# Two-block gated cross-attention network: another order of the engines' work in the fused last stage, and other PSUM banks for two transposes

## The reference, cut to what matters

```python
# attention: 16 heads of 64, scores over the 64 rows of the same sequence's context
fq, fk, fv = q @ w_q, k @ w_k, v @ w_v            # q is layernorm(x); k, v are the context
ps = softmax(fq fk^T / 8 + mask)
x = x + tanh(g) * ((ps fv) @ out_w.T + out_b)
# feed-forward
xq = round(x_n * scale) / scale                   # scale = 127 / max|x_n| of the row, x_n = layernorm(x)
h  = silu(depthwise_conv3(xq @ w1q.T))            # along the 64 rows; 512 hidden features
x  = x + tanh(g) * (quantised(h) @ w2q.T)         # h is rounded by its own row's step
```

## Time and profile before

| | before |
|---|---|
| three executions, us | 1636.68, 1643.49, 1648.65 |
| profiled execution, us | 1640.07 |
| span of it, us | 1637.7 |
| PE busy, share of the span | 92% |
| DVE busy | 72% |
| ACT busy | 61% |
| POOL busy | 42% |
| the fused stage | from about 752 us to the end |

### The profile page before, as it was taken

One profiled execution on the slowest core, in us unless ns is written; L12 is line 12 of the kernel. 1 busy time (PEld: TensorE's weight loads), 2 busy tenths in 40 slices (PEclk: granted clock), 3 DMA queues, 4 the chain that ended last, 5 costly groups with the idle time before them and its releaser, 6 DMA issues.

```text
span 1637.7 us, 51409 instructions
## 1 busy us (share of the span) xinstructions
PE 1505.6 (92%) x20222; PEld 1246.3 (76%) x20222; DVE 1174.8 (72%) x3120; ACT 995.8 (61%) x2018; POOL 692.5 (42%) x611
## 2 busy tenths in 40 slices
PE   5999999999839999997899999999999999999988
PEld 2777777777729999986677777777787878888864
DVE  5788878876544222234587989889898899888875
ACT  3787777766214444443456566766666667767756
POOL 2234667575441111144565454444444444333320
PEclk9899999987559999998999999999999999999999
DMA  9999950000038888861000000000000000000000
GB/s 299 393 387 386 382 196 24 24 31 21 27 113 257 263 267 262 255 196 39 26 23 18 18 17 22 24 22 22 23 23 22 22 22 22 12 16 12 14 9 23
DMA packets 97661, 173.36 MB, mean 106 GB/s; under 512 B 12320, under 2 KB 44960, under 8 KB 97168
## 3 DMA queue, kind: packets, MB, share of 16 engines
q1 hardware_dynamic: 84816, 144.05, 26.3%
q0 software_dynamic: 11600, 25.65, 4.6%
q10 hardware_dynamic: 1008, 0.40, 0.1%
HBM read 79.41 MB, written 90.64 MB: 104 GB/s over the span
## 4 chain that ended last, share of the span: by engine, by line
PE 39%; DVE 8%; issue 4%; ACT 1%; POOL 1%; another core or an unknown queue 0%; DVEq 0%; ACTq 0%
PE L1psY L1283 6%; PE L1psY L1290 6%; PE L1psM L1332 5%; PE L1psY L1275 5%; PE L1psT L1324 4%; PE L1psS L1301 4%; PE L1psT L1310 2%; DVE L1sc L1708 1%; PE L1psF L1380 1%; PE L1psF L1361 1%; PE L1psF L1398 1%; DVE L1den L1719 1%; DVE L1am L1770 1%; PE L1psM L1390 1%; DVE x L1600 1%
## 5 line engine op out<-in xcount | busy, mean ns | idle before, releaser
L1851 POOL TENSOR_TENSOR L1sc<-L1sc,L1top 128x1024 f32<-128x1024 f32 x64 | 121.8, 1904 | 240.8 <-DVE L1top L1715 240.8
L1463 ACT ACTIVATE L1KT<-L1psY 128x512 f32<-128x512 f32 x128 | 78.0, 609 | 226.7 <-PE L1psY L1275 216.9
L1004 ACT ACTIVATE GhT<-GpsH,Gwx 128x256 f32<-128x256 f32 (+1 forms) x312 | 117.9, 445 | 149.9 <-PE GpsH L972 143.6
L855 POOL TENSOR_TENSOR L0sc<-L0sc,L0top 128x1024 f32<-128x1024 f32 x64 | 121.6, 1900 | 178.6 <-DVE L0top L564 177.7
L1856 POOL TENSOR_TENSOR L1sc<-L1sc,L1rden 128x1024 f32<-128x1024 f32 x64 | 121.8, 1904 | 177.0 <-DVE L1rden L1724 177.0
L1283 PE MATMUL L1psY<-L1xnT,L1WQ 128*128 128x128 f32 x1024 | 142.8, 283 | 1.0 <-ACT L1xnT L1458 1.0
L1021 DVE TENSOR_TENSOR yg<-GpsY,Gwx 128x256 f32<-128x256 f32 (+1 forms) x78 | 30.3, 389 | 158.0 <-PE GpsY L980 84.9
L861 POOL DMA_INDIRECT rows_in<-L0xr,slot x128 | 124.5, 972 | 45.3 <-issue 31.8
L1275 PE MATMUL L1psY<-cx,L1WK 128*128 128x128 f32 x1024 | 138.4, 279 | 2.6 <-DVE L1identh L1791 2.5
L980 PE MATMUL GpsY<-Gwx,GhT 128*128 128x128 f32 x1080 | 133.1, 275 | 0.0
L980 PEld LDWEIGHTS GpsY<-Gwx,GhT 128*128 128x128 f32 x1080 | 130.9, 192 | 2.7
(11 more groups left out here) (326 smaller groups left out, 3732.4 us busy)
## 6 DMA issues: line engine op xcount, KB each, us to landing
Gwx<-in_experts SPq DMA_DIRECT2D x78, 579.0 KB, 4.3
rows_in<-L0zero SPq DMA_DIRECT2D x1, 33792.0 KB, 92.7
rows_out<-L0zero SPq DMA_DIRECT2D x1, 33792.0 KB
Gxg<-rows_in SPq DMA_DIRECT2D x57, 128.0 KB, 3.8
rows_out<-yg POOLq DMA_DIRECT2D x57, 128.0 KB
cx<-in_ctxT SPq DMA_DIRECT2D x64, 64.0 KB
out<-X SPq DMA_DIRECT2D x64, 64.0 KB, 1.7
L0ctxT<-in_ctxT SPq DMA_DIRECT2D x1, 2560.0 KB, 18.6
```

The costliest lines, as they stand in the source:

```text
L855: nc.gpsimd.tensor_tensor(sc[:, t % 4, :, :], sc[:, t % 4, :, :], top[:, t % 2, :].unsqueeze(2).broadcast_to([P, H, S]), ALU.subtract).the ...
L1004: nc.scalar.activation(hT[:, u, m, 0:blocks(t) * P], psH[:, u, m, 0:blocks(t) * P], ACT.Gelu, bias=wx[:, w, ob1 + m:ob1 + m + 1]).then_inc ...
L1851: nc.gpsimd.tensor_tensor(sc[:, t % SR, :, :], sc[:, t % SR, :, :], broad(top[:, t % 2, :]), ALU.subtract).then_inc(s["shifted"], 1)
```

## The change

Nothing is computed differently. In the fused stage five things change.

- ScalarE: `exps` moves ahead of both `take_probs`, which now stand together behind it. `centre` goes behind the first `take_q`, and `tanh` ahead of the second `take_o`.
- VectorE: `add_x`, `largest` and `scales` open the next round instead of closing this one (the neighbours stay the same, as the rows below show). `residual` goes behind `add_bias` instead of ahead of it, `scale` ahead of `layernorm`, and `layernorm` behind `sums` and `invert`. The last three portions of small steps stand behind `twice_silu`.
- GpSimd: `fetch` stands behind `normalise` in every round. Before, this was so only in rounds 0 to 5.
- TensorE: `turn_xq` and `turn_steps` of the 14 groups in integers write into the two banks of the scores (`psS`) instead of `psM` and `psF`, and stand behind `project_out`. They wait for `add_bias` of the round, and the next `scores` waits for ScalarE's copies of both.
- TensorE: `project_out` waits for the halves of its input one by one.

```diff
             if stage == "xq":
-                return ("M", psM[:, 2:4, :]) if t // G4 < INT_GROUPS else ("F", psF[:, :])
+                return ("S", flat(psS[:, 0, :, :])) if t // G4 < INT_GROUPS else ("F", psF[:, :])
+            if stage == "steps":
+                return "S", flat(psS[:, 1, :, :])
...
             def scores(t):
                 pe.wait_ge(s["q_ready"], 2 * t + 2)
                 wait(pe, s["scores_out"], t)
+                g = min((t + LX - FX - 1) // G4 + 1, INT_GROUPS)
+                wait(pe, s["xqT_ready"], g)
+                wait(pe, s["steps_ready"], g)
...
             def project_out(t):
-                pe.wait_ge(s["OT_ready"], 2 * t + 2)
                 take_bank("M", s["x_new"], t + 1)
                 for i in range(HP):
+                    if i % 4 == 0:
+                        pe.wait_ge(s["OT_ready"], 2 * t + i // 4 + 1)
...
             def turn_xq(g):
...
-                take_bank(name, s["xqT_ready"], g + 1)
                 if g < INT_GROUPS:
+                    pe.wait_ge(s["scores_out"], min(G4 * g + FX - LX + 1, NT))
                     ps = halves(ps, BF16)
+                else:
+                    take_bank(name, s["xqT_ready"], g + 1)
...
# TensorE's loop
-                if k >= FX and (k - FX) % G4 == 0 and k - FX < NT:
+                if k >= FX and (k - FX) % G4 == 0 and INT_GROUPS <= (k - FX) // G4 < NG:
                     turn_xq((k - FX) // G4)
-                if k >= FX and (k - FX) % G4 == 0 and (k - FX) // G4 < INT_GROUPS:
-                    turn_steps((k - FX) // G4)
                 if tt is not None:
                     project_out(tt)
+                if k >= FX and (k - FX) % G4 == 0 and (k - FX) // G4 < INT_GROUPS:
+                    turn_xq((k - FX) // G4)
+                    turn_steps((k - FX) // G4)
...
# ScalarE's loop
-                if tt is not None:
-                    take_probs(tt, 0)
                 if tile(k - 1, FT) is not None:
                     rounding(tile(k - 1, FT))
                 if tx is not None:
                     take_xnT(tx)
+                if tv is not None:
+                    exps(tv)
                 if tt is not None:
+                    take_probs(tt, 0)
                     take_probs(tt, 1)
                 if tx is not None:
                     take_k(tx, 1)
-                if tv is not None:
-                    exps(tv)
...
# GpSimd's loop
-                if k >= 6:
-                    for t in fetches.get(k, []):
-                        fetch(t)
                 if tv is not None:
                     normalise(tv)
-                if k < 6:
-                    for t in fetches.get(k, []):
-                        fetch(t)
+                for t in fetches.get(k, []):
+                    fetch(t)
```

More of the change, by code:

```diff
@@ L1349, in turn_steps @@
                 pe.wait_ge(s["xq_ready"], g + 1)
-                take_bank("F", s["steps_ready"], g + 1)
+                ps = bank("steps", G4 * g)[1]
                 for i in range(G4):
                     t = G4 * g + i
-                    last = nc.tensor.transpose(psF[:, i * P:(i + 1) * P], inv[:, t:t + 1].broadcast_to([P, P]), ident[:])
+                    last = nc.tensor.transpose(ps[:, i * P:(i + 1) * P], inv[:, t:t + 1].broadcast_to([P, P]), ident[:])
                 last.then_inc(s["steps_ps"], 1)
@@ L1502, in take_steps @@
                 wait(act, s["h_scaled"], FM * (g - 1))
-                nc.scalar.activation(step[:, g % 2, :], psF[:, :], ACT.Copy).then_inc(s["steps_ready"], 1)
+                nc.scalar.activation(step[:, g % 2, :], bank("steps", G4 * g)[1], ACT.Copy).then_inc(s["steps_ready"], 1)
             def centre(n):
@@ L1552, in _ @@
                     take_k(tx, 1)
-                if tv is not None:
-                    exps(tv)
+                if tx is not None:
+                    take_q(tx, 0)
                 if n is not None:
                     centre(n)
-                if tx is not None:
-                    take_q(tx, 0)
                 if tt is not None:
@@ L1562, in _ @@
                     take_q(tx, 1)
+                if n2 is not None:
+                    tanh(n2)
                 if tt is not None:
                     take_o(tt, 1)
-                if n2 is not None:
-                    tanh(n2)
                 if tb is not None:
@@ L1794, in _ @@
                 n, n2, th, tb = tile(k, FH), tile(k, FH + 1), tile(k, FT), tile(k, FB)
+                if tile(k - 1, LT) is not None:
+                    add_x(tile(k - 1, LT))
+                if tile(k - 1, FT) is not None:
+                    largest(tile(k - 1, FT))
+                    scales(tile(k - 1, FT))
                 if to is not None:
@@ L1799, in _ @@
                 small(k, 0)
+                if n is not None:
+                    scale(n)
+                small(k, 1)
+                if tv is not None:
+                    sums(tv)
+                    invert(tv)
                 if tile(k, LN) is not None:
@@ L1802, in _ @@
                 if n is not None:
-                    scale(n)
-                small(k, 1)
-                small(k, 2)
-                if tv is not None:
-                    sums(tv)
-                    invert(tv)
-                if n is not None:
                     conv_left(n)
                     conv_right(n)
-                small(k, 3)
                 if n2 is not None:
                     twice_silu(n2)
+                small(k, 2)
+                small(k, 3)
                 small(k, 4)
+                if tx is not None:
+                    add_bias(tx)
                 if tb is not None:
@@ L1818, in _ @@
                 if tx is not None:
-                    add_bias(tx)
                     tops(tx)
-                if tt is not None:
-                    add_x(tt)
-                if th is not None:
-                    largest(th)
-                    scales(th)
+            add_x(NT - 1)
+            largest(tile(LAST - 1, FT))
+            scales(tile(LAST - 1, FT))
             LAST_NORM = {50: range(11, 18), 51: range(18, 23), 52: range(23, FFN_OPS)}
```

## The result

| | before | changed |
|---|---|---|
| median (lowest to highest) | 1641.5 us (1636.7 to 1648.7), 4 runs | 1693.4 us (1686.9 to 1701.3), 4 runs |
| span of the profiled execution | 1637.7 | 1688.4 |
| ratio | | 1.031 (1.027 to 1.035) |

The account below looks back on a forecast made before the run. TensorE bounds the kernel, 12.07 us a tile plus waits. Middle: -23.1 - 7.2 + 11.6 + 37.4 = +18.7; nine tiles before +7.1, 14 behind +2.2: +28 on 1640.07, predicted 1667 us, range 1620 to 1690 (own range 1655 to 1685).

Parts of the forecast that it names:

- The step that failed: Fused stage, tiles 0 to 5: given no term in the sum, so predicted difference 0.
- The tail: Fused stage, tile 63 to the end: given no term in the sum, so predicted difference 0.
- Gathers on the scores: Middle tiles: both gathers now hit the scores, 1.1 us each in 34 tiles, +37.4 us (30 to 79).
- Gathers away from `values`: Middle tiles: gathers issued behind `normalise` no longer interrupt `values`, 0.89 us off 26 tiles, -23.1 us.
- `exps` ahead of the copies: ScalarE: copies of the probabilities end later, `values` starts at 4.53 instead of 4.19; 34 tiles at 0.34, +11.6 us.
- Banks for integers and steps: Middle's eight turning rounds: the steps' wait for `residual` goes, 1.6 us becomes 0.7 each, -7.2 us.
- the shorter way to the maxima: VectorE, `residual` behind `add_bias`: maxima end about 2.75 us after the scores instead of 3.19.
- Rival 3: VectorE's `twice_silu` delays the gathers 0.7 us, hitting scores for 1.8 us instead of 1.1: +30, 1697 us; 5%.
- the rule: Skill's shared-port rule: gathers beside `twice_silu` would come later and longer; left out of the sum as not borne out.
- Rivals 1, 2 and 4: Scores not hurt, 1624 us, 22%; price about half a microsecond, 1641 us, 17%; gathers and ScalarE's order free, 1604 us, 4%.
- rival 4: Fused stage: neither the gathers nor ScalarE's order cost anything, `exps` having unseen slack; 1604 us; 4%.

## Why the prediction was right in direction and wrong in size

With the two kernels on both kinds of chip the difference splits into what small matmuls lose to gathers (hurt chip less spared chip) and the rest (changed less before, spared chip). These are single profiles of different chips; the second changed profile on a hurt chip repeats the first one within 0.6 us a stretch.

| us | tiles 0 to 5 | 6 to 14 | 15 to 48 | 49 to 62 | 63 to the end |
|---|---|---|---|---|---|
| before, spared chip | 70.6 | 104.4 | 433.8 | 175.1 | 79.2 |
| changed, spared chip | 73.6 | 110.1 | 437.2 | 177.2 | 81.2 |
| the rest | +3.0 | +5.7 | +3.4 | +2.1 | +2.0 |
| gathers, before | 7.2 | 6.2 | 12.3 | -0.8 | -2.5 |
| gathers, changed | 19.9 | 8.9 | 30.9 | 0.0 | -0.6 |

The last two columns have few gathers or none; their differences show how far two chips or profiles differ anyway.

**The step that failed** is the one that isn't in the sum: the prediction starts its parts at tile 6 and takes the first six tiles as unchanged, without a reason. They cost +15.7 us, over two thirds of what the forecast (28) fell short of the measured 50.7. GpSimd gathers four times a round there. The place of these gathers in its own order is the same in both kernels; it is the other engines' new order that brings them forward, from 10.2 us or more of the tile to 7.7 to 8.1 in tiles 3 and 4, so that they lie on the scores from their start. Scores of 3.5 to 4.7 us stand in three of the six tiles, where the earlier trace rows show the one such case before (the stage's first tile has 6.4 us before and 6.5 now). The waits were accompanied by the granted clock's falls, 34 us at the lower level instead of 10. Of the 15.7, 12.7 are gathers and the clock with them: on the spared chip the changed kernel's mean granted clock is 0.95 in these tiles, on the two hurt ones 0.82 and 0.85. On one hurt chip the same kernel takes 92.9 us there with gathers and 69.9 with plain DMAs at their place. Which engine's order brings them forward was not separated on a hurt chip. The miss of 22.7 us is these 15.7, the tail's 4.0, also not in the sum, and 5.2 in the parts that were in it, less 2.2 us by which the part ahead of the stage was shorter. (The sum itself gives 1640.07 + 28.0 = 1668 us; the prediction has 1667.)

The tail, too, stood at nothing. In the round that drains the pipeline `values` waits for the late copy, and behind that idle time the clock is at its lower level for 3.4 us, and again later for 6.8 (`values` takes 1.99 us at it instead of 1.16):

```profile
1624.76 1.99 PE L1329 MATMUL L1psT<-L1PT,L1V 64*64 64x64 f32 x64 [1.67 <-ACT L1PT L1493]
```

**Gathers on the scores**: predicted for every tile, 1.1 us each. Right: they hit in every one of tiles 15 to 48. The price is about 1.0, 1.1, 1.8 (or 1.4) and 0.9 (or 0.7) in the four kinds of round, 1.13 on average, 38.5 us in all. The plain tile is 13.5 us with gathers and 12.46 without, as forecast (13.5 and 12.4). GpSimd's pair runs from 7.7 to 10.0 us in a plain tile (8.2 to 10.4 in the forecast). The largest price is in the round in which it ends 1.1 us later (11.14).

**Gathers away from `values`**: predicted -23.1, a loss counted by adding the gaps of 26 tiles. The measurement is -12.3: on the spared chip, with every `values` whole, the kernel before still needs 433.8 us. Its four kinds of round are 12.06, 12.07, 12.6 or 13.2, and 14.05 to 14.3 us there; without the gap in `values` the third kind is no shorter (12.91 us on average, 12.95 on the hurt chip) and the fourth gains 0.5 of the 0.9 (14.13, 14.62), so something else ends those tiles, and the gap had lain in that wait. The same is seen on the scores: the gaps add up to 38.5 us, close to the forecast's 37.4, but the difference between the chips is 30.9. The two errors were +10.8 and -6.5 us; that the middle came out at +22.0 against +18.7 owes something to their cancelling.

**`exps` ahead of the copies**: predicted 0.34 a tile, measured 0.40 (`values` at 4.59, not 4.19), TensorE's largest named wait in the middle (19.2 us of idle time at 34 places). ScalarE's whole new order, alone on a spared chip, costs 13.4 us there, predicted 11.6.

**Banks for integers and steps**: predicted -7.2 in the middle. The turning tile gains 0.45 of the 0.9 and on a hurt chip gives most of it back to `values` one tile later. VectorE's order was given no price of its own beyond the shorter way to the maxima; the whole of it, alone, costs 7.8 us in the middle and 6.4 in tiles 49 to 62. In the changed kernel the three together are +3.4, about the +4.4 that the prediction had for them, and far less than the 21.2 us that the two orders cost one by one: each is cheaper beside the other.

**Rival 3, gathers held back by `twice_silu`.** The forecast called it not borne out by the trace. It exists, at a smaller price; that the measured 1693 us lies near this rival's 1697 is a coincidence. GpSimd's gathers and VectorE's `twice_silu` in the changed kernel, first GpSimd, then VectorE:

```profile
1150.04 1.26 POOL L1878 DMA_INDIRECT yr<-rows_out,slot  x1
...
1205.03 1.32 POOL L1878 DMA_INDIRECT yr<-rows_out,slot  x1
```

```profile
1149.44 1.00 DVE L1773 SCALAR_TENSOR_TENSOR L1hs<-L1hs,L1hc 128x512 f32<-128x512 f32 x1
...
1204.80 0.69 DVE L1773 SCALAR_TENSOR_TENSOR L1hs<-L1hs,L1hc 128x512 f32<-128x512 f32 x1 [0.29 <-ACT L1hs L1526]
...
1287.85 0.69 DVE L1773 SCALAR_TENSOR_TENSOR L1hs<-L1hs,L1hc 128x512 f32<-128x512 f32 x1 [0.38 <-ACT L1hs L1526]
```

Where `twice_silu` has begun before the gather (1149.44 against 1150.04, 1204.80 against 1205.03) the gather lasts 1.25 to 1.33 us and ends 0.85 to 0.9 behind `twice_silu`; where it begins during the gather (1287.85 against 1287.60, the tile above) the gather lasts 0.98. That is 9 of the 34 rounds, at some 0.3 us: about 3 us, inside the prices above. The Trainium skill (SBUF — State Buffer, "SBUF: two separate sides") says less than the prediction made of it: whichever of the two engines starts first holds the shared port pair, VectorE work with two SBUF inputs contends only against a GpSimd operation that reads SBUF, and it is VectorE's two-port modes that keep descriptors from being written. The trace agrees on the order of starting: the indirect gather is longer only where VectorE is already at it, and by 0.3 us, not the 0.7 that I had made of it. The row with which the prediction set the rule aside was of the other case: `collect`'s second step began at 1258.49, 0.03 us after the gather.

Rivals 1, 2 and 4 needed scores that a gather hurts little or not. On the hurt chips that is excluded by every tile of the middle. On a spared chip it holds, and the change still is 1.4% slower (1.008 to 1.021). ScalarE's wait of 0.40 us a tile, which rival 4 denied, is there too. How the rest divides between the two orders and the gathers is open, as the 1.003 without gathers shows.

## What to carry to other kernels

A stretch that is given no change in a sum has to be argued like any other: the ramp at a pipeline's start has other counts (here four gathers a round instead of two), and here its waits came with a lower granted clock. A gap seen in a timeline is worth its length only where nothing else ends the same round; adding it up over all rounds overstates both gain and loss. Where small matmuls are hurt, put what hurts them (here an indirect gather) beside large matmuls by a wait of its own, a gather at a time, rather than by its place between two other passes.

## What the runs showed of the hardware that I had not expected

- Five measurements of the kernel before fall into two groups: 1641, 1664 and 1645 us, and 1586 and 1587 us on two other chips. In the first group 64 small matmuls beside GpSimd's indirect gathers take from 1.3 us, where one grazes them, to 4.7 us, and over 6 in the stage's first tile; in the second 1.16 to 1.26 beside the same gathers. Why, these runs don't tell; nor whether it belongs to the chip, for each chip was used in one sitting.
- The hurt in the fused stage is only half of the difference between the groups. Of 47.1 us between the two profiles of the kernel before, 24.6 lie ahead of the stage. That part is the same in all versions; it takes 744 to 770 us in the profiles of hurt chips and 718 to 730 in those of spared ones. It was not looked into.
- Where it happens, it takes an indirect DMA: plain DMAs from the same engine at the same place leave the scores at 1.16 us, even four in a row on top of them.
- The loss grows with lateness of the gather against the scores: 1.1 us when the pair ends 1.1 us after their start, 1.8 when 2.3 after, and in the version with the copies first 2.0 when 2.4 after and 2.4 when 2.9 after. Lateness is not all of it: where the pair ends 2.1 after, three tiles lost 1.4, one 1.5 and one 0.8. The loss reaches past the last small matmul into short bf16 ones.
